# One buffer of one-hot columns instead of two, rebuilt in quarters behind TensorE

## The reference, cut to what matters

```python
kj = k[src] + e
alpha = jnp.einsum('ehc,ehc->eh', q[dst], kj) / jnp.sqrt(jnp.float32(C))
amax = jax.ops.segment_max(alpha, dst, num_segments=n)
ex = jnp.exp(alpha - amax[dst])
denom = jax.ops.segment_sum(ex, dst, num_segments=n)
w = ex / (denom[dst] + 1e-16)
msg = (v[src] + e) * w[:, :, None]
out = jax.ops.segment_sum(msg, dst, num_segments=n).reshape(n, D)
```

## Time and profile before

| what | value |
|---|---|
| device time, median of 3 runs | 3183.93 us (3182.84 to 3184.53) |
| profiled execution, span from first to last instruction | 3640.5 us |
| GpSimd busy | 2015.5 us, 55% |
| TensorE matmuls busy | 2313.1 us, 64% |
| VectorE busy | 1974.9 us, 54% |
| ScalarE busy | 1172.0 us, 32% |
| DMA engines, mean rate over the span | 106 GB/s |

### The profile page before, as it was taken

How to read it: one execution, slowest core, us unless ns; L and a number is a source line. 1 busy time by engine, 2 the same in 40 slices (tenths; PEclk the granted TensorE clock), 3 DMA queues, 4 the chain that set the end, 5 groups by cost and what they waited for, 6 DMA issues and landing times. The chain is left out here.

```text
span 3640.5 us, 67503 instructions
## 1 busy us (share of the span) xinstructions
PE 2313.1 (64%) x14712; PEld 1806.8 (50%) x14713; DVE 1974.9 (54%) x5388; ACT 1172.0 (32%) x3723; POOL 2015.5 (55%) x2306
## 2 busy tenths in 40 slices
PE   5567999726666666666666681666566666666660
PEld 3335999515455455545555441455454555454550
DVE  5554222326556556656566652566566665565666
ACT  1001555303333333333333430233333333333343
POOL 3500222346666666666666267466666666666637
PEclk6656999856656666556565665565666656666665
DMA  7787111223333333333335113233333333333342
GB/s 206 213 262 213 37 37 37 77 79 108 110 111 108 103 104 110 110 109 111 103 107 94 26 46 117 79 110 111 109 111 109 100 109 111 109 111 104 104 44 71
DMA packets 276049, 384.84 MB, mean 106 GB/s; under 512 B 121804, under 2 KB 207772, under 8 KB 275676
## 3 DMA queue, kind: packets, MB, share of 16 engines
q0 software_dynamic: 80768, 220.05, 21.6%
q1 hardware_dynamic: 145628, 163.04, 14.2%
q10 hardware_dynamic: 49536, 0.55, 0.8%
HBM read 360.42 MB, written 23.02 MB: 105 GB/s over the span
## 5 line engine op out<-in xcount | busy, mean ns | idle before, releaser
L1351 POOL DMA_INDIRECT wide<-kv,a_source x1664 | 1691.0, 1016 | 922.7 <-issue 470.9
L1385 PE MATMUL psum<-wide,a_hot 128*128 128x136 f32 x3328 | 855.4, 416 | 391.5 <-issue 215.7
L1374 PE MATMUL psum<-wide,a_hot_t 128*128 x4992 | 697.9, 287 | 511.3 <-issue 333.4
L1579 DVE TENSOR_TENSOR acc<-acc,psum 128x136 f32 x1664 | 488.8, 294 | 914.5 <-remote 681.8
L1385 PEld LDWEIGHTS psum<-wide,a_hot 128*128 128x128 f32 x3328 | 695.8, 292 | 513.1 <-issue 317.3
L1374 PEld LDWEIGHTS psum<-wide,a_hot_t 128*128 128x128 bf16 x4992 | 516.3, 115 | 678.6 <-issue 591.7
L1441 ACT ACTIVATE a_edge_q<-psum 128x16 f32<-128x16 f32 x416 | 74.6, 180 | 1770.8 <-remote 1379.9
L1449 ACT ACTIVATE a_hot<-iota_n,a_spot 128x128 f32<-128x128 f32 x1664 | 526.5, 390 | 25.3 <-PE psum L1385 12.6
L1498 DVE TENSOR_TENSOR a_product<-psum,wide 128x512 f32<-128x512 f32 x416 | 284.6, 684 | 178.1 <-remote 85.0
L1453 ACT ACTIVATE a_hot<-a_hot,ones 128x512 f32<-128x512 f32 x416 | 300.2, 722 | 13.6
L1501 DVE TENSOR_REDUCE a_score<-a_product 128x16 f32<-128x512 f32 x416 | 286.4, 688 | 14.4
(11 more groups left out here) (263 smaller groups left out, 2257.5 us busy)
## 6 DMA issues: line engine op xcount, KB each, us to landing
acc<-in_edge_attr SPq DMA_DIRECT2D x344, 192.0 KB, 3.5
a_place<-places SPq DMA_DIRECT2D x104, 512.0 KB
wide<-kv,a_source POOLq DMA_INDIRECT x1664
kv<-acc SPq DMA_DIRECT2D x49, 128.0 KB
kv<-p_pairs SPq DMA_DIRECT2D x49, 128.0 KB
c_node<-drec ACTq DMA_DIRECT2D x344, 1.5 KB
a_cut<-breaks SPq DMA_DIRECT2D x208, 8.1 KB
acc<-in_x SPq DMA_DIRECT2D x49, 64.0 KB
```

The source lines that it names most:

```text
L1351: pool.indirect_dma_start(out=ring[:, at.b, n, :], out_offset=None, in_=kv[:, :], in_offset=bass.IndirectOffsetOnAxis(ap=source[at.b][:, n ...
L1374: last = pe.matmul(query_out(q)[:, t, :], hot_t[:, b, q * QUAD + t, :], rows, start=(s == 0), stop=(s == SPLIT - 1), skip_group_check=True)
L1385: last = pe.matmul(sum_out(q, t), hot[q % 2][:, t, :], ring[:, (at.b + back) % 2, q * QUAD + t, LEAD:KV], start=True, stop=True, skip_grou ...
L1579: dve.tensor_tensor(here, here, sum_out(q, t), ALU.add).then_inc(added, 1)
```

## The change

`hot_t` loses its second half. The columns of a turn are made in four quarters of 8 tiles (two quads) instead of two halves of 16. In turn g, VectorE makes quarter 0, 1, 2, 3 for turn g + 1 at the end of steps 1, 3, 5 and 7, over the quarter that TensorE has used by then: when VectorE begins step s it has already waited for the matmuls of quad s. SP reloads half 0 of `place` after quarter 1 (step 3) and half 1 after quarter 3 (step 7), both for turn g + 2. As the first column of a turn is overwritten in step 1, ScalarE copies it in step 0 into one of two new tiles, `begin`, and VectorE waits for that copy before it makes quarter 0. TensorE waits on `made_hot` before every second quad.

```diff
-        hot_t = sb("hot_t", [P, 2, G, P], BF16)
+        hot_t = sb("hot_t", [P, G, P], BF16)
+        begin = [sb(f"begin{b}", [P, 1]) for b in (0, 1)]
...
+        PARTS = QUADS // 2
+        PART = G // PARTS
...
                 if at.has(-1):
-                    at.wait(made_hot, 2, 2)
-                    load_places(g + 1, 1)
                     at.wait(multiplied, QUADS, 0)
                     load_source(g + 1, other)
                     at.wait(linked, LINKS, SUNK - LINKS)
                     load_cuts(g + 1, other)
+                if at.has(-2):
+                    at.wait(made_hot, PARTS, PARTS + PARTS // 2)
+                    load_places(g + 2, 0)
+                if at.has(-1):
                     at.wait(linked, LINKS, SHARED - LINKS)
                     load_weight(g + 1, other)
                 if at.has():
                     at.wait(hot_there, QUADS, -QUADS)
                     load_spots(g, at.b)
                 if at.has(-2):
-                    at.wait(made_hot, 2, 3)
-                    load_places(g + 2, 0)
+                    at.wait(made_hot, PARTS, 2 * PARTS)
+                    load_places(g + 2, 1)
...
-            sp.wait_ge(made_hot, 1)
-            load_places(1, 0)
+            for h in (0, 1):
+                sp.wait_ge(made_hot, (h + 1) * PARTS // 2)
+                load_places(1, h)
...
-                if q % (QUADS // 2) == 0:
-                    at.wait(made_hot, 2, q // (QUADS // 2) + 1 + 2 * later)
+                if q % 2 == 0:
+                    at.wait(made_hot, PARTS, q // 2 + 1 + PARTS * later)
...
-                        last = pe.matmul(query_out(q)[:, t, :], hot_t[:, b, q * QUAD + t, :], rows, start=(s == 0),
+                        last = pe.matmul(query_out(q)[:, t, :], hot_t[:, q * QUAD + t, :], rows, start=(s == 0),
...
-                act.activation(begins[:, :], hot_t[:, b, 0, 0:1], ACT.Copy).then_inc(columns, 1)
-                at.wait(columns, 2, 0)
-                act.activation(decay[:, :], drop_out, ACT.Exp, scale=begins[:, 0:1]).then_inc(decayed, 1)
+                at.wait(columns, 1, 0)
+                at.wait(begin_there, 1, 0)
+                act.activation(decay[:, :], drop_out, ACT.Exp, scale=begin[b][:, 0:1]).then_inc(decayed, 1)
...
+                    if s == 0 and at.has():
+                        act.activation(begin[at.b][:, :], hot_t[:, 0, 0:1], ACT.Copy).then_inc(begin_there, 1)
...
-            def make_hot(at, later, h):
+            def make_hot(at, later, part):
+                h, here = part * PART // HALF, part * PART % HALF
                 at.wait(place_in[h], 16, 16 + 16 * later)
-                dve.tensor_scalar(hot_t[:, (at.b + later) % 2, h * HALF:(h + 1) * HALF, :].rearrange("p t e -> p (t e)"),
-                                  place[h][:, :], lane[:, 0:1], None, ALU.is_equal).then_inc(made_hot, 1)
+                dve.tensor_scalar(hot_t[:, part * PART:(part + 1) * PART, :].rearrange("p t e -> p (t e)"),
+                                  place[h][:, here * P:(here + PART) * P], lane[:, 0:1], None, ALU.is_equal
+                                  ).then_inc(made_hot, 1)
...
-                    if s >= QUADS - 2 and at.has(-1):
-                        make_hot(at, 1, s - QUADS + 2)
+                    if s % 2 == 1 and at.has(-1):
+                        if s == 1:
+                            at.wait(begin_there, 1, 1)
+                        make_hot(at, 1, s // 2)
...
-            for h in (0, 1):
-                make_hot(Turn(dve, 0), 0, h)
+            for part in range(PARTS):
+                make_hot(Turn(dve, 0), 0, part)
```

More of the change, by code:

```diff
@@ L1258, in attend_stage @@
         drop = spare[:, 3 * HEADS * WIDTH:3 * HEADS * WIDTH + HEADS]
-        column, begins, decay = (m["pick"][:, at:at + n] for at, n in ((0, 2), (2, 1), (3, HEADS)))
+        column, decay = (m["pick"][:, at:at + n] for at, n in ((0, 2), (3, HEADS)))
         source_in, weight_in, spot_in, place_in, cut_in = ([sem(f"{n}{b}") for b in (0, 1)] for n in (
@@ L1264, in attend_stage @@
         (cleared, made_hot, products, multiplied, reduced, edge_there, apart, hot_there, weighted, added, linked,
-         columns, decayed, grown, begun) = (sem(n) for n in (
+         columns, decayed, grown, begun, begin_there) = (sem(n) for n in (
             "cleared", "made_hot", "products", "multiplied", "reduced", "edge_there", "apart", "hot_there", "weighted",
-            "added", "linked", "columns", "decayed", "grown", "begun"))
+            "added", "linked", "columns", "decayed", "grown", "begun", "begin_there"))
+        PARTS = QUADS // 2
+        PART = G // PARTS
         block = inner.enter_context(nc.Block())
@@ L1362, in queries @@
             def queries(at, later, q):
-                b = (at.b + later) % 2
                 if q <= 2 or q % 2 == 0:
```

## The result

| | median of 12 runs | lowest to highest |
|---|---|---|
| before | 3185.23 us | 3179.73 to 3193.41 |
| changed | 3189.52 us | 3184.21 to 3196.95 |

The ratio is 1.0017, with a 95% interval of 1.0009 to 1.0024. So the change costs about 5 us (0.17%): under the 0.2% that I took as the bound to "no change", but on the other side of zero from the 14 us gain that I forecast. A second measurement of the changed kernel gave 1.0008 (1.0000 to 1.0017), which just touches no change. The time lies within the stated range of 3148 to 3203; the direction was wrong.

What follows compares the result with a forecast made beforehand. The prediction took GpSimd's gather queue as the bound. Fewer `make_hot` collisions gained 14 us, all other terms 0: 3184 - 14 = 3170 us, its own range 3143 to 3177, and 3148 to 3203 for 8 in 10.

Steps and rivals of the forecast that it cites:

- The gather queue sets the pace: GpSimd's 1664 gathers run nearly without a stop in a timed run, at a cadence of 1.254 us, 2087 us in all.
- The 441.9 us of GpSimd's waits: GpSimd's idle time waiting for TensorE's steps in the profile, taken as an effect of the recording and absent from timed runs.
- TensorE's waits cost nothing: TensorE's 102.4 us of waits for the half made in step 6 go, costed at nothing as hidden under the gather queue.
- Rival 3: VectorE and TensorE bound the timed run too, so TensorE's 102.4 us of waits come off: 3082 us; chance 0.06.
- What `make_hot` costs: Gathers starting during `make_hot` are lengthened; quarters collide less than halves, gaining 8 to 22 us, taken as 14 us.
- the weighting, a term put at nothing: Gathers lengthened by the weighting, more than half of the 104 us over the median, had no reason to grow.
- hidden under the 10 us it has below GpSimd: VectorE's four quarters add 0.22 us a turn, costing nothing under GpSimd's longer turn; 11 us without this cover.
- rival 1: No change that can be told: fewer hits by quarters, more by the weighting; 3184 us, 3178 to 3190; chance 0.28.
- Rival 2: Slower, 3205 us: four locked quarters each hit gathers, 0.76 us a turn against 0.33, +21 us; chance 0.20.
- The costs put at nothing: ScalarE's `begin` copy in step 0 and SP's reordered `place` loads: priced 0; 10 us if late, 4.5 us a turn uncovered.

Runs made afterwards that it cites:

- the kernels of the table: Follow-up kernels and repeats, variants of before or changed, each timed against before; ratios from 0.9907 to 1.0048.
- the added reductions: Kernel before plus one VectorE reduction of 0.41 us, its result not used, in each of steps 1, 3 and 5: 3201.29 us, ratio 1.0048.

## Why the prediction was wrong

**The gather queue sets the pace: right.** In the undisturbed profiles of before and of the changed kernel (its first) the gathers of a layer run without a gap over 0.4 us, 1069.7 us in layer 0 and 1078.0 in layer 1 of the changed kernel; in each other profile there are at most seven such gaps, 4.3 us in sum. Their busy sum goes from 1615 to 1653 us over the kernels of the table, while the span less that sum stays between 1537 and 1548. The 441.9 us of GpSimd's waits were the recording's.

**TensorE's waits cost nothing: right.** 187.6 us of waits for the columns became 20.9, and no time came of it. Rival 3, with 3082 us, is out.

**What `make_hot` costs: right in sign, and half the size.** I had 0.33 us a turn for halves with starts at random, 0.66 with starts that follow the rows, and took the middle. Measured are 16.2 us in 50 turns, the random value (16.5). For quarters I had 8 to 10.5 us, and 8.0 to 10.2 were measured. The term is a gain of 6 to 8 us, where I took 14. The higher count was read from the stretched execution, and for that one it was right: its `make_hot` lengthens the gathers by 32.4 us, 0.65 us a turn. Its weighting does so by 69.5 us, and of its 104 us over the median 56 are left in the undisturbed profile. So the mistake was to take the places of instructions, and not only their durations, from an execution that its recording had moved. A quarter takes 0.492 us and not 0.43, so VectorE's work grows by 101.8 - 82.3 = 19.5 us, 0.38 us a turn instead of 0.22.

**The step that failed: the weighting, a term put at nothing.** I costed VectorE's longer work as "hidden under the 10 us it has below GpSimd", and said of the weighting against rival 1 that "that part has no reason to grow". Both look at a turn as a whole, on the mean. Measured are 11 to 14 us more under the weighting, against the 6 to 8 us that `make_hot` gives back. That the place of the quarters does it (SP's order of loads went with it) is shown by the same quarters made late: the weighting is back at 33 us, the time 9.3 us lower with two buffers, and 0.4 to 0.5% lower with one. The place tells in steps 5 and 6, where VectorE starts its products later (medians of 2.51 and 2.28 us in layer 0, against 1.99 and 1.91 with one buffer and quarters late) and the weighting's excess is 8.8 to 10.0 us in place of 0.3 to 1.7. The growth in steps 2 and 4 of layer 0 came in every kernel with quarters, wherever they were made. The standing still at the loop's start alone doesn't give it: before with two more instructions has 5.3 us there, not 11 to 13. Its cause stays open, and so does how much of the changed kernel's 3 to 5 us comes from the standing still.

**The rivals.** Rival 1 had the mechanism: fewer hits by the columns, more by the weighting; it gave 3178 to 3190 us, and 3189.5 came. Rival 2 had the side, but not the cause: quarters cost 0.16 to 0.20 us a turn in all (8.0 to 10.2 us in 50 turns) and not 0.76, and split alone they gain.

**The costs put at nothing** (`begin` in step 0, SP's loads in another order) show no sign: no wait at them stands among the large ones, and the kernel with one buffer and quarters late has `begin` too and is the fastest of those that leave the weighting where it was. The changed kernel's order of SP's loads was not run apart from the place.

## What to carry to other kernels

Where one engine's queue sets the pace, work off that path is not free because its engine has room on the mean: ask at which moments it meets the queue, and take the steps one by one, as a step that got longer makes the ones behind it late. When an edit moves instructions that lock or delay another engine, sum the cost of all such instructions, not only of those that the edit touches; here the larger part belonged to one that it left alone, and moving that one was worth 28 us. A profile whose span is far over the timed runs should be taken again before its idle times, or what meets what in it, are read.

## What the runs showed of the hardware

An elementwise product of two operands in SBUF (the weighting, 128x512 f32, 0.68 us) lengthens an indirect gather that starts during it, from 0.95 to as much as 1.50 us, by what is left of it less 0.11 us, where more is left than that. The rule holds within 0.05 us for all 166 gathers that start in a weighting in before's second profile and for 211 of 217 in the changed kernel's. A gather that runs already is not lengthened (1122.16 above). The Trainium skill ("SBUF — State Buffer", § Who interferes with whom) says that such an instruction contends with GpSimd's reads, but infers that it leaves the generation of descriptors alone. These gathers are lengthened; as they also read their row numbers (`source`) from SBUF, no run here tells whether it is by that read or by the descriptors. By the same section a reduction never contends on this chip; the trace agrees: of the 74 gathers that started in the added reductions (0.41 us each) none was lengthened.

In the other direction I had read from one row that VectorE's instruction keeps its 0.75 us where a gather came first. Over the 104 halves of the second profile the mean is 793 ns against 752, and single ones take up to 0.98 us: some are lengthened, by less than the rest of the gather.

Four or more further VectorE instructions in a pass of the loop turned 6 fetches of code into 56 in layer 0, with 3.3 us of standing still behind each branch; one more recorded event in a pass (359, one buffer with halves) did not. In layer 1 both kernels fetch at every pass, and there VectorE's sequencer stands 2.8 to 3.0 us behind the branch before, too.
